# Node pass: LayerNorm roots by Newton steps on VectorE; third GAT layer: own rows added by identity products on TensorE

## The reference

```python
h = relu(layernorm(x))
x = x + gat3(h)              # three GAT layers
h = relu(layernorm(x))
x = x + net3(h)              # three message passing layers

# a GAT layer m; every node also has a loop edge to itself
hw = x @ W[m];  s = hw @ a_src[m];  d = hw @ a_dst[m]
e = leaky_relu(s[src] + d[dst], 0.2)
alpha = softmax of e over the edges of each destination
x = x + sigmoid(segment_sum(alpha * hw[src], dst) + b[m])

# a message passing layer
e = relu(concat(x[src], x[dst], e_before) @ We + be)
x = relu(concat(x, segment_sum(e * edge_weight, dst)) @ Wn + bn)
```

## Time and profile before

| | |
|---|---|
| median of 3 runs | 6300.57 us (6300.21 to 6308.27) |
| the profiled execution's own time | 6295.87 us |
| its span in the trace | 6294.3 us |
| mean granted TensorE clock | 0.919 of 2.4 GHz |
| busy share of the span | PE 80%, DVE 70%, ACT 58%, POOL 68% |
| node pass in the span | about 63 to 1958 us |
| third GAT layer | about 3400 to 4065 us (the second about 2780 to 3395) |

### The profile page before, as it was taken

The page is one execution under the profiler, slowest core; times in us unless marked ns, Lnnn a source line. Parts: engine busy times, 40 slices in busy tenths (PEclk is TensorE's granted clock), DMA queues, the critical chain, the costliest instruction groups (busy, mean ns, idle before and its releaser), DMA issues. The chain is left out here.

```text
span 6294.3 us, 106455 instructions
## 1 busy us (share of the span) xinstructions
PE 5015.9 (80%) x23702; PEld 3013.2 (48%) x23702; DVE 4383.7 (70%) x12187; ACT 3632.4 (58%) x7888; POOL 4266.9 (68%) x4317
## 2 busy tenths in 40 slices
PE   4999999999984637765885777699989996776765
PEld 2666666666651224433442444366656663333332
DVE  6888888888865868876885899856645554444443
ACT  4999999999885926654664466633323332333332
POOL 4777777788860077747774776177767766777777
PEclk9999999999997968886887888899999998999998
DMA  6888888887764646655764788667767774444442
GB/s 196 272 276 276 285 277 277 273 237 232 230 189 153 211 131 198 201 160 162 207 201 128 240 265 260 227 211 222 222 207 236 236 223 138 130 131 127 130 123 89
DMA packets 873559, 1288.67 MB, mean 205 GB/s; under 512 B 291334, under 2 KB 344295, under 8 KB 866635
## 3 DMA queue, kind: packets, MB, share of 16 engines
q1 hardware_dynamic: 730450, 1051.72, 49.8%
q0 software_dynamic: 142688, 232.29, 15.6%
HBM read 634.34 MB, written 654.88 MB: 205 GB/s over the span
## 5 line engine op out<-in xcount | busy, mean ns | idle before, releaser
L1381 POOL DMA_INDIRECT g_xs<-table,g_gi x1176 | 1209.9, 1029 | 889.3 <-DMA g_gi<-in_src_lookups_dram 349.2
L1675 POOL DMA_INDIRECT n_xs<-table,n_gi x1176 | 1205.2, 1025 | 567.3 <-issue 346.8
L1818 DVE TENSOR_TENSOR_SCAN n_dT<-n_km,n_dT,bank 128x512 f32<-128x512 uint8 x291 | 372.3, 1279 | 998.9 <-PE bank L1703 980.6
L1778 ACT ACTIVATE n_eT<-bank,edge_b 128x512 f32<-128x512 f32 x294 | 202.2, 688 | 809.4 <-PE bank L1720 804.7
L709 PE MATMUL bank<-n_zT,wn 128*128 128x512 f32 (+1 forms) x1176 | 540.9, 595 | 77.6 <-issue 71.0
L690 PE MATMUL bank<-n_xT,gat_w 128*128 128x512 f32 (+1 forms) x1176 | 545.4, 600 | 21.0 <-ACT n_xT L759 18.4
L1686 POOL DMA_INDIRECT out_dram<-n_xn,n_eo x392 | 427.4, 1090 | 125.2 <-issue 116.1
L630 POOL DMA_INDIRECT node_map<-p_es x392 | 402.1, 1026 | 119.5 <-issue 114.1
L658 POOL DMA_INDIRECT p_lk<-node_map,p_gi x392 | 394.5, 1006 | 122.8 <-issue 107.9
L625 POOL DMA_INDIRECT p_rows<-in_x_dram,p_es x392 | 393.2, 1003 | 124.5 <-issue 109.9
L863 DVE COPY n_ro<-bank 128x512 f32<-128x512 f32 (+1 forms) x392 | 252.6, 685 | 311.9 <-PE bank L719 274.9
(11 more groups left out here) (263 smaller groups left out, 12521.5 us busy)
## 6 DMA issues: line engine op xcount, KB each, us to landing
table<-n_ro SPq DMA_DIRECT2D x768, 256.0 KB
g_gb<-decays SPq DMA_DIRECT2D x294, 256.0 KB, 4.2
n_xd<-table SPq DMA_DIRECT2D x294, 256.0 KB
table<-g_xn SPq DMA_DIRECT2D x196, 256.0 KB
g_xo<-table SPq DMA_DIRECT2D x196, 256.0 KB
edge_feats<-n_eT SPq DMA_DIRECT2D x196, 256.0 KB, 2.9
table<-n_xn SPq DMA_DIRECT2D x196, 256.0 KB, 3.0
n_ea<-edge_feats SPq DMA_DIRECT2D x196, 256.0 KB
```

The source lines that it names most:

```text
L1381: q.indirect_dma_start(out=xs[g % XR][:, u, :], out_offset=None, in_=tables[l], in_offset=bass.IndirectOffsetOnAxis(ap=gi[g % 6][:, 0, u:u ...
L1675: q.indirect_dma_start(out=xs[g][:, u, :], out_offset=None, in_=tables[L], in_offset=bass.IndirectOffsetOnAxis(ap=gi[g][:, u, slot_word:sl ...
L1818: V.tensor_tensor_scan(in_order(dT[g][:, :]), kept(g), in_order(flat_banks[1]), 0.0 if begins(g) else carry(dT[g.before(1)]), ALU.mult, AL ...
```

## The change

It has two parts.

**Node pass.** The square root on ACT and the reciprocal on DVE are gone. Both LayerNorms of a macro step (the one of macro S and the one of macro S - 4) lie side by side in one tile, and DVE makes one over the root for both at once: eight instructions over 32 columns (`scales`, at the end of the step that closes a macro), then three rounds of three instructions (`newton`, spread over the next step: before `stats`, between `rows_of` 0 and 1, between `zrows_of` 0 and 1), then the shift (`shifts`, one instruction before `zrows_of` 2). `seen` makes DVE wait for its own last instruction. The statistics are held in two tiles, the scales in three.

**Third GAT layer.** `add_self` no longer waits for ACT's `scale`. It is one product of the 512 columns of own rows with the four shares, broadcast, into a new tile `xv`. `turn` does for each tile two products with the identity that add up in PSUM, one of `xw` and one of `xv`, in place of one transpose.

```diff
-def unrolled(eng, groups, work, un):
+def unrolled(eng, groups, work, un, longer=()):
...
-            if 0 <= s - lag + low < groups:
+            if 0 <= s - lag + low < groups + (LN_LAG if fn in longer else 0):
...
-                    unrolled(a, GT, [(1, root(ln1, sc1)), (17, root(ln2, sc2))]
-                             + [(LAG_P[m], gate(m)) for m in range(3)]
+                    unrolled(a, GT, [(LAG_P[m], gate(m)) for m in range(3)]
...
+                    def scales(g):
+                        if not closes(g):
+                            return
+                        S_ = g.c // MG
+                        t, s = tiles_of(S_)
+                        v.wait_ge(done1, min(GT, max(0, (S_ - NSC + 1) * MG))) if S_ >= NSC else None
+                        if S_ >= NSC + LN_LAG // MG:
+                            v.wait_ge(done2, (S_ - NSC + 1) * MG - LN_LAG)
+                        seen()
+                        step(V.tensor_tensor(s[0], t[:, :, :, 1], t[:, :, :, 4], ALU.subtract))
+                        step(V.tensor_tensor(s[1], t[:, :, :, 2], t[:, :, :, 5], ALU.add))
+                        step(V.tensor_tensor(s[3], t[:, :, :, 1], t[:, :, :, 4], ALU.add))
+                        seen()
+                        step(V.tensor_tensor(s[0], s[0], s[0], ALU.mult))
+                        step(V.tensor_scalar(s[1], s[1], 1.0 / C, EPS, ALU.mult, ALU.add))
+                        seen()
+                        step(V.scalar_tensor_tensor(out=s[1], in0=s[0], scalar=0.25, in1=s[1], op0=ALU.mult, op1=ALU.add))
+                        seen()
+                        step(V.tensor_scalar(s[2].bitcast(i32), s[1].bitcast(i32), 1, None, ALU.logical_shift_right))
+                        seen()
+                        step(V.tensor_scalar(s[2].bitcast(i32), s[2].bitcast(i32), -1.0, float(0x5F3759DF), ALU.mult, ALU.add))
...
+                    def newton(g):
...
+                        step(V.tensor_tensor(s[0], s[2], s[2], ALU.mult))
+                        seen()
+                        step(V.scalar_tensor_tensor(out=s[0], in0=s[0], scalar=-0.5, in1=s[1], op0=ALU.mult, op1=ALU.mult))
+                        seen()
+                        step(V.scalar_tensor_tensor(out=s[2], in0=s[0], scalar=1.5, in1=s[2], op0=ALU.add, op1=ALU.mult))
+                        seen()
...
-                             + [(0, stats(ln1, xm, st1, sc1, x_ld))]
-                             + [(LAG_B[m], rows_of(m)) for m in range(3)]
-                             + [(16, stats(ln2, mid, st2, sc2, None))]
-                             + [(LAG_ZB[m], zrows_of(m)) for m in range(3)]
-                             + [(1, scales(ln1, sc1)), (17, scales(ln2, sc2))], UN)
+                             + [(1, newton), (0, stats(0, xm, x_ld))]
+                             + [(LAG_B[0], rows_of(0)), (1, newton), (LAG_B[1], rows_of(1)), (LAG_B[2], rows_of(2))]
+                             + [(16, stats(1, mid, None)), (LAG_ZB[0], zrows_of(0)), (1, newton), (LAG_ZB[1], zrows_of(1)),
+                                (1, shifts), (LAG_ZB[2], zrows_of(2)), (0, scales)], UN, (scales, newton, shifts))
...
                         def add_self(g):
+                            if last_layer:
+                                landed(v, ol, g)
+                                ready(v, turned, g - 1)
+                                i = g % SG * U
+                                V.tensor_tensor(xv[g % 2][:, :, :], xo[g % OR][:, :, :],
+                                                cols[g // SG % 2][:, 1, i:i + U].unsqueeze(2).broadcast_to([P, U, P]),
+                                                ALU.mult).then_inc(selfed, 1)
+                                return
...
                             pe.wait_ge(selfed, g + 1)
                             ready(pe, summed, g - 1)
+                            if last_layer:
+                                pe.wait_ge(scaled, g + 1)
+                                for u in range(U):
+                                    T.matmul(banks[g % 2][:, u, :], lhsT=xw[g % 3][:, u, :], rhs=ident[:, :],
+                                             start=True, stop=False, skip_group_check=True)
+                                    last = T.matmul(banks[g % 2][:, u, :], lhsT=xv[g % 2][:, u, :], rhs=ident[:, :],
+                                                    start=False, stop=True, skip_group_check=True)
+                                last.then_inc(turned, 1)
+                                return
```

More of the change, by code:

```diff
@@ L37 @@
 NEWTON = 3
+LN_LAG, NSC = 16, 3
 NF = 8
@@ L521, in slot_rows @@
             return t[ds(g.at(P * U), P * U), :].rearrange("(p u) c -> p u c", p=P)
-        ln_stages = ("stats", "sums", "squares", "var", "root", "rstd", "shift", "done")
         x_ld = sems("x_loaded", MR)
-        ln1 = {k: sem(f"nodes_norm_{k}") for k in ln_stages}
-        ln2 = {k: sem(f"mid_nodes_norm_{k}") for k in ln_stages}
+        norm_step, shifted, done1, done2 = (sem(k) for k in ("norm_step", "norm_shifted", "nodes_normed", "mid_nodes_normed"))
         h_st, g_st, r_st = sems("h_stored", 2), sems("h2_stored", 2), [sems(f"rows_stored{m}_", 2) for m in range(5)]
@@ L540, in build @@
             xm, mid = macro_tiles("n_xm", [P, MU, C]), macro_tiles("n_mid", [P, MU, C])
-            st1, st2 = macro_tiles("n_st1_", [P, MU, 6]), macro_tiles("n_st2_", [P, MU, 6])
-            sc1, sc2 = macro_tiles("n_sc1_", [P, 6, MU]), macro_tiles("n_sc2_", [P, 6, MU])
+            st = [sb(f"n_st{k}", [P, 2, MU, 6], f32, c2) for k in range(2)]
+            sc = [sb(f"n_sc{k}", [P, 4, 2, MU], f32, c2) for k in range(NSC)]
             h, zr = ring("n_h", 2), ring("n_zr", 2)
@@ L595, in store @@
                         return fn
-                    unrolled(sp, GT, [(-3, load), (5, store(tables[0], h, ln1["done"], h_st)),
+                    unrolled(sp, GT, [(-3, load), (5, store(tables[0], h, done1, h_st)),
                                       (9, store(tables[1], ro[0], d_rw[0], r_st[0], NODE0)),
                                       (11, store(tables[2], ro[1], d_rw[1], r_st[1], NODE0)),
-                                      (21, store(tables[3], zr, ln2["done"], g_st, NODE0)),
+                                      (21, store(tables[3], zr, done2, g_st, NODE0)),
                                       (24, store(tables[4], ro[2], c_rw[0], r_st[2], NODE0)),
@@ L723, in _, with apply @@
                              + [(LAG_B[m], back(m)) for m in range(3)]
-                             + [(6, enter(banks[0], h, ln1["done"], d_c0, d_t0))]
+                             + [(6, enter(banks[0], h, done1, d_c0, d_t0))]
                              + [(LAG_ZP[m], zproduct(m)) for m in range(3)]
                              + [(LAG_ZB[m], zback(m)) for m in range(3)]
-                             + [(22, enter(banks[1], zr, ln2["done"], c_c0, c_t0))], UN)
+                             + [(22, enter(banks[1], zr, done2, c_c0, c_t0))], UN)
                 @block.scalar
                 def _(a):
-                    def root(z, sc):
+                    def apply(k_, done, rows, to, landed, entered):
                         def fn(g):
-                            if closes(g):
-                                t = of_macro(sc, g)
-                                a.wait_ge(z["var"], macro(g).count())
-                                S.activation(t[:, 3, :], t[:, 2, :], ACT.Sqrt).then_inc(z["root"], 1)
-                        return fn
-                    def apply(z, sc, rows, to, landed, entered):
-                        def fn(g):
-                            p, t = parts(g), of_macro(sc, g)
-                            a.wait_ge(z["shift"], macro(g).count())
+                            p, t = parts(g), scales_of(g, k_)
+                            a.wait_ge(shifted, g.c // MG + k_ * LN_LAG // MG + 1)
                             if g.i is not None or g.c >= 2:
@@ L797, in fn @@
                                 v.wait_ge(d_rw[2], g.count())
[L798 to L800 removed]
                             of = group_of(of_macro(rows, g), g)
+                            p = parts(g)
                             for k in range(U):
[L803 to L817 removed]
@@ L818, in stats @@
-                        return fn
-                    def scales(z, sc):
-                        def fn(g):
-                            if closes(g):
-                                n, s = macro(g).count(), of_macro(sc, g)
-                                v.wait_ge(z["root"], n)
-                                V.reciprocal(s[:, 4, :], s[:, 3, :]).then_inc(z["rstd"], 1)
-                                v.wait_ge(z["rstd"], n)
-                                V.scalar_tensor_tensor(out=s[:, 5, :], in0=s[:, 0, :], scalar=-0.5, in1=s[:, 4, :],
-                                                       op0=ALU.mult, op1=ALU.mult).then_inc(z["shift"], 1)
-                        return fn
```

(14 more changed lines are left out.)

46 lines of the change are left out of this document (21 added, 25 removed).

## The result

The changed kernel takes 6217.09 us (median of 4 runs, 6211.5 to 6225.94), the kernel before 6301.99 us (median of 4, 6300.21 to 6308.27). The ratio is 0.9865, 95% interval 0.9848 to 0.9882: 85 us less. The forecast was 6219.

The account below looks back on a forecast made before the run. PE, stalled behind ACT's table loads, was taken to bound the node pass, and DVE the third layer. Gains of 70 (81 + 7 - 18) and 10 (15 - 5) sum to 80 us: 6219 us, range 6186 to 6258.

Parts of the forecast that it names:

- (a): Node pass, ACT: table loads and roots go, PE's stall with them; 81 us, plus 7 at the start.
- (b): Node pass, DVE: eight instructions take 1.8 us or less, all 18 4.0 a macro; DVE fits on average.
- (c): Node pass: Newton rounds before rows_of make PE's zback wait 0.4 us a macro, 18 us given back (0 to 54).
- R2: Rival, node pass: Newton in DVE's queue costs PE more than 0.4 a macro; at 1.2, 6255 us; chance 0.17.
- (e): End of node pass: POOL doesn't cut the gain; stores pace the end, DMA counted at 0 to 10 us.
- (g): Third layer, PE: eight products take 2.0 us, a group 4.96; DVE waits 1.9 a chain, 15 us net gain.
- (h): Third layer's tail: the last dozen groups run at PE's pace, 5 us lost (0 to 15).
- (i): Third layer, POOL's gathers: 5.31 us a group, not the bound, but capping the layer's gain near 37.
- R1: Rival, third layer: PE doesn't bind, its clock stays up, 30 us or more gained; about 6195 us; chance 0.14.
- R4: Rival, slower than before: PE's half clock takes hold in the third layer; at clock 0.70, 6345 us; chance 0.03.
- R3: Rival, third layer: a float32 identity product costs four times a transpose, 155 us lost there; 6385 us; chance 0.01.
- R5: Rival, node pass: roots on ACT were hidden by something else, so that node stays; about 6290 us; chance 0.02.

Follow-up runs that it names:

- own_rows_not_turned: Changed kernel with PE's turn in the third layer as four transposes of scaled rows alone, own rows left out of the sum: 6201.37 us in one run.
- roots_without_table: Kernel before with ACT's Copy in place of Sqrt in the node pass's LayerNorms, nothing new on DVE: 6215.76 us in one run.
- stores_split_again: Changed kernel with the node pass's last 106 row stores split into 96 and 10, run again; own time not given, the first time 7957.21 us, ratio 0.9895.
- the kernel with all three edits: Changed kernel with second Newton round behind the second statistics, last stores split, and third layer own rows partly back on DVE; fastest of its session, time not given.

## Why the prediction was right, step by step

The mechanisms were those forecast: the table loads' stall goes, a smaller wait of zback comes, and PE takes back a part of DVE's saving. The sum was 80 us (70 + 10) and the result 80.3 in the phases (65.3 + 15.0). Not each term was right.

- **(a) The stall of the first z product: right.** Between the first and the last gate of the node pass there were 100 table loads, and now there is none. The copy in place of the root gave the full 8.65 step and a macro of 34.59. At the start of the pass I gave 7 us. When the steps have settled (the twentieth x product), the changed kernel is 5.3 us ahead (185.5 against 190.8), the kernel whose roots cost nothing 12.3 (178.5). Other profiles of the same node passes have 193.1 for the pass before and 184.3 and 184.4 for the changed one, so 5.3 is the low end of 5 to 9. So the start held more than I estimated. The 6 to 7 that the changed kernel doesn't get I put down to the longer Newton chain, priced at 2 in (d); no run takes it apart.
- **(b), (c) Newton on DVE: right.** A round 0.67 (0.66 forecast), the eight 1.52 ("1.8 or less"), the new wait 0.39 (0.4), the macro 34.98 (35.0), in the forecast place. The runs with the round moved and doubled show the cause. R2, a wait of 1.2, falls.
- **ACT below 125 of 150: wrong.** It is 132.3. Four macros fit into 150 us, so 12 us had to go from 138.8, which gives 126.7 and so not quite the 125 that I wrote; but the window now holds 36.4 / 34.98 as many of them, which makes 131.9. I forgot that step.
- **(e) The end of the pass: right in kind.** The stores pace it; from the last z product to the edges it is 49.7 us, and was 49.5 (1912.9 to 1962.4). The DMA's 0 to 10 us were at most some 3: over 41 settled macros the changed kernel's exceed 34.98 by 3.2 us in all, the late ones at 35.1 to 35.3; what holds those I don't know. That the 49.7 is mostly the price of a 106 row store I had seen in the rows and not asked after.
- **(f) DVE's saving: right.** Four additions 1.05, the product 0.61 from its start to the next one's, forecast 0.60; the chain without PE's part 39.9 (39.95).
- **(g) PE's eight products: right in price, too dear in effect.** 1.88 us (2.0) and 4.91 a group (4.96). But DVE waits 1.2 a chain, not 1.9, and the chain is 41.14, not 41.9: the idle time behind the long step shrank from 4.87 to 2.95, and the half clock behind it cost 1.44 (6.35 - 4.91) instead of 2.66; I had carried both over unchanged. From the first to the last of the fourteen scans the change gains 20.3 us (553.4 to 533.2), not 15. The wait is in the softmax's first step, one of the two places named.
- **(h) The tail: right.** From the last scan to the end of the layer 78.4 us before, 83.5 after: 5.1 lost, 5 forecast (6.5 against the other two kernels with the old layer). The mixed kernels, whose last eight groups DVE adds as before, have it back at 78.2 to 79.2.
- **(i) POOL's cap of 37: wrong.** The kernel that doesn't turn the own rows gained 40.5, with PE out of the way. I had taken 5.31 us a group from the second layer as the least; nothing in the rows said that POOL was at its limit there. The figure has a slip in it, too: 7 x 5.31 = 37.2 us would be the length of a chain at POOL's pace. As a gain that is 43.1 - 37.2 = 5.9 a chain, 83 over fourteen, so even taken as a limit it lies beyond the ceiling of 44 and caps nothing.

So 15 - 5 was 20.3 - 5.1, and 70 was 65.3: the start gave 5.3 for 7, the way from there to the last z product 60.2 for 63 (1722.1 to 1661.9 us), the drain lost 0.2. The node pass gave 5 less and the layer 5 more, and that these offset each other is luck. So is a total within 2 us of 6219: the medians fell by 85 us, the spans of the two profiles by 79. What kept the terms near was that each big term had a row of its own shape: the 8.65 us step that was there three times in four, and four float32 products in 1.00.

R1 (PE doesn't bind in the third layer) falls by own_rows_not_turned: PE takes 25.5 us there. R4 falls with a clock of 0.95. R3 falls too: had each product cost four times a transpose's 0.15, the eight would take 4.8, and they take 1.88; four transposes of the same size took 0.60. A turned float32 tile cost 0.15 us as a transpose and 0.235 as a product (1.88 / 8). The factor of four that the Trainium skill gives in TensorE: Matmul & The Clock Gate, section Terms, is not borne out by these rows. R5 falls by roots_without_table.

## What to carry to other kernels

A function whose table is loaded and unloaded again costs two loads in the queue of everything behind it: here 2.9 us once a macro, 1.81 of it on PE. Before such work moves to another engine's queue, look for the place in that queue where nobody waits, since one round of 0.67 us costs all or nothing by where it stands. And when a sum is moved onto TensorE, count what PE gives back: here 25.5 of 40.5 us, shown by DVE's waits on PE. In the tail, where PE's group of 4.91 us is longer than DVE's step, moving it cost 5 us, and leaving the last eight groups where they were gave it back. Whether fewer groups moved would pay within the chains too, no run here shows.

## What the hardware showed that I had not expected

A store of 106 partitions (212 KB) occupied SP's queue for 4.3 us; split into 96 and 10 partitions it took two issues of 0.4 to 0.5 us each in most cases (0.74 for two, 1.87 for four), and the stretch behind the last z product fell from 49.4 to 12.2 us. Size alone isn't the cause: stores of 128 rows (256 KB), in the middle of the changed kernel's pass, took SP mostly 0.33 to 0.46 us each:

```profile
1001.74 0.34 SPq L595 DMA_DIRECT2D table<-n_zr  x1
...
1003.16 0.40 SPq L595 DMA_DIRECT2D out_dram<-n_ro  x1
```

The windows of the end of the pass, in the columns of the earlier trace rows, of the changed kernel and of stores_split_again:

```profile
1865.00:1880.00 15.00, 1.07 (x4) 0.67 (x4) 0.69 (x1) 0.00 (x0) 0.00 (x0) 0.50 0.14 52
```
```profile
2657.00:2667.00 10.00, 5.84 (x37) 3.91 (x34) 5.58 (x9) 1.85 (x4) 0.00 (x0) 0.94 0.65 207
```

The 106 row stores kept 0.14 of the 16 DMA engines busy, about two of them, at 52 GB/s; split, 0.65 at 207. The Trainium skill, DMA: Bandwidth & Descriptors, section "Why a DMA increments its semaphore by 16 and not by 1", says that a DMA goes over the largest number of engines, up to 16, that divides its slowest dimension. For 106 that is 2, for 96 it is 16 and for 10 it is 10; the shares agree.

The two later chips moved less while POOL gathered. The same window of the node pass, the kernel with all three edits, with POOL at work and after it has ended:

```profile
900.00:1050.00 150.00, 70.33 (x170) 32.29 (x171) 30.91 (x80) 30.93 (x59) 118.00 (x132) 0.59 0.33 104
2000.00:2150.00 150.00, 150.00 (x768) 98.89 (x767) 134.60 (x378) 133.39 (x277) 0.00 (x0) 1.00 0.71 242
```

And what each DMA queue moved from 900 to 1050 us, there and in the kernel before on the first chip (packets, MB, share):

```profile
q0 software_dynamic: 4825, 7.22, 17.7%
q1 hardware_dynamic: 4170, 8.38, 15.2%
```
```profile
q1 hardware_dynamic: 17150, 34.38, 62.6%
q0 software_dynamic: 4753, 7.21, 21.9%
```

POOL's queue moved the same 7.2 MB in both, SP's a quarter of what it did. POOL's own time was the same too (118.0 and 118.6 of 150 us). The kernel before was some 1740 and 1800 us longer there, and the others likewise. Why these chips share so unevenly between the two queues no run here tells.
